# A wide convolution in an eight-sample audio network: three outputs from five products instead of two from four, with the side work of GpSimd and VectorE put in another order

## The reference, cut to what matters

```python
logits = conv1d_same(gelu(conv1d_same(xt, rc_w1, rc_b1)), rc_w2, rc_b2)    # the router
...
sh = conv1d_same(xt, sh_w1, sh_b1)        # 9 taps, 128 -> 512 channels
sh = jax.nn.silu(sh)
sh = conv1d_same(sh, sh_w2, sh_b2)        # 1 tap, 512 -> 128 channels
z = residual + y + sh.transpose(0, 2, 1)
return layer_norm(z) * ln_g + ln_b
```

## Time and profile before

| | us |
|---|---|
| median of 3 runs | 1534.27 |
| lowest, highest | 1530.68, 1536.31 |
| profiled execution, its own time | 1544.43 |
| its span in the trace | 1542.6 |
| TensorE busy (10360 records) | 1305.9, 85% of the span |
| VectorE busy | 1003.6, 65% |
| ScalarE busy | 644.9, 42% |
| GpSimd busy | 699.3, 45% |
| mean granted clock of TensorE | 0.92 |

### The profile page before, as it was taken

How to read it: one execution, slowest core, us unless ns; L and a number is a source line. 1 busy time by engine, 2 the same in 40 slices (tenths; PEclk the granted TensorE clock), 3 DMA queues, 4 the chain that set the end, 5 groups by cost and what they waited for, 6 DMA issues and landing times.

```text
span 1542.6 us, 33397 instructions
## 1 busy us (share of the span) xinstructions
PE 1305.9 (85%) x10360; PEld 1103.2 (72%) x10361; DVE 1003.6 (65%) x3235; ACT 644.9 (42%) x1610; POOL 699.3 (45%) x1055
## 2 busy tenths in 40 slices
PE   6696777787899937778899899988998989999974
PEld 3464646564899935556788778876887989999953
DVE  4467768665466656757863786467663628989946
ACT  1346272523122204335335453445334436666623
POOL 0112556444688853133531444242614526777732
PEclk9697989898999978989999899999998999999987
DMA  6000400003588840010010001000100237777725
GB/s 191 4 21 6 111 27 22 25 21 95 161 266 256 263 170 1 2 42 1 24 61 0 2 14 58 14 1 1 43 1 8 95 97 191 196 194 198 196 88 161
DMA packets 102202, 128.46 MB, mean 83 GB/s; under 512 B 21015, under 2 KB 61181, under 8 KB 101842
## 3 DMA queue, kind: packets, MB, share of 16 engines
q1 hardware_dynamic: 88786, 102.36, 23.1%
q0 software_dynamic: 13312, 24.74, 4.8%
HBM read 96.13 MB, written 34.94 MB: 85 GB/s over the span
## 4 chain that ended last, share of the span: by engine, by line
PE 60%; DVE 15%; issue 7%; DVEq 6%; POOL 5%; ACT 4%; DMA 2%; POOLq 0%; SPq 0%; ACTq 0%
PE psum L980 12%; PE psum L1133 11%; PE psum L989 9%; DVE work L1554 3%; PE psum L1142 3%; PE psum L1047 2%; POOL rows_in L2130 2%; PE psum L1094 2%; PE psum L1072 2%; PE psum L794 2%; PE psum L1191 2%; PE psum L969 2%; PE psum L1018 2%; DVE stats L1537 2%; PE psum L1067 1%
## 5 line engine op out<-in xcount | busy, mean ns | idle before, releaser
L1133 PE MATMUL psum<-NT,wreg 128*128 128x182 f32 (+1 forms) x1536 | 261.6, 326 | 10.2 <-ACT pack L1434 5.1
L1133 PEld LDWEIGHTS psum<-NT,wreg 128*128 128x128 f32 x1536 | 247.9, 192 | 18.9 <-ACT pack L1434 5.9
L2162 POOL DMA_INDIRECT rows_out<-work,expert_row_kept x208 | 206.2, 992 | 79.6 <-issue 41.1
L980 PE MATMUL psum<-work 128*128 128x128 f32 x1664 | 222.7, 277 | 0.9 <-ACT work L1336 0.9
L980 PEld LDWEIGHTS psum<-work 128*128 128x128 f32 x1664 | 203.9, 193 | 1.7 <-issue 0.9
L2111 POOL TENSOR_TENSOR rstd<-var_eps,pack 128x6 f32<-128x6 f32 x40 | 56.5, 1415 | 215.0 <-DVE var_eps L1544 214.9
L1329 ACT ACTIVATE work<-psum,work 128x128 f32<-128x128 f32 x416 | 118.6, 368 | 64.4 <-PE psum L980 64.3
L1876 DVE SCALAR_TENSOR_TENSOR work<-psum,work 128x128 f32<-128x128 f32 x416 | 117.1, 344 | 7.7
L794 PE MATMUL psum<-pack,work 128*128 128x128 f32 (+2 forms) x288 | 51.4, 336 | 82.0 <-DVE work L1554 75.5
L1885 DVE TENSOR_SCALAR work<-psum,expert_row_kept 128x128 f32<-128x128 f32 x208 | 72.8, 350 | 71.8 <-PE psum L969 36.6
L2130 POOL DMA_INDIRECT rows_in<-N,slot_now x96 | 100.5, 1046 | 28.6 <-issue 28.4
(11 more groups left out here) (364 smaller groups left out, 2894.3 us busy)
## 6 DMA issues: line engine op xcount, KB each, us to landing
work<-w_and_b SPq DMA_DIRECT2D x104, 258.0 KB
work<-in_ew SPq DMA_DIRECT2D x104, 256.0 KB
work<-rows_in SPq DMA_DIRECT2D x208, 65.0 KB
work<-rows_out SPq DMA_DIRECT2D x32, 384.0 KB, 4.2
rows_out<-work,expert_row_kept POOLq DMA_INDIRECT x208
work<-in_xT SPq DMA_DIRECT2D x8, 375.0 KB, 3.0
w_and_b<-in_ew SPq DMA_DIRECT2D x1, 2560.0 KB
out<-H SPq DMA_DIRECT2D x8, 320.0 KB
```

The costliest lines, as they stand in the source:

```text
L980: r_ = mm(v.ps1[:, c * P:(c + 1) * P], v.w1[:, c * P:(c + 1) * P], v.xT, start=True, stop=True)
L1133: r = mm(bank[:, half * HALF_PAIRS:half * HALF_PAIRS + p1 - p0], weights[:, m * P:(m + 1) * P], product_input(name, g, k, p0, p1), start=( ...
L2162: G.indirect_dma_start(rows_out[m], bass.IndirectOffsetOnAxis(ap=v.dest, axis=0), v.y, None, bounds_check=last, oob_is_err=False).then_inc ...
```

## The change

What it does, part by part:
- **Products.** For one group of three taps, three neighbouring outputs come from five products on a third of the columns. A unit is now one sample (748 outputs, 250 triples) and one block of hidden channels, thus 8 units. It is made of three fills: p12 (6 matmuls of 250 columns), p03 (6) and p4 (3). Fills take the two PSUM banks in turn.
- **Combination.** Seven operations of 250 columns on VectorE (four, a drain, three), where part p03 of the next unit stands. ACT copies 500, 500 and 250 columns, and silu works on 748 columns at once.
- **Rows.** Both halves of a sample are multiplied after its fourth block. Those of lane 1 stand at the end of an iteration.
- **Fills.** `FILL` changes at the end of the list, and parts are weighted by cost (6, 6, 3, and 4 for rows).
- **Input and weights on GpSimd.** `turn` becomes twelve operations, one of 504 and eleven of 252 columns, with three drains. `make_conv_weights` becomes eight operations of 1536 columns.
- **GpSimd's order.** The norm powers of norm5 come first in an iteration, and `turn` of lane 1 stands at the end of its own iteration. The norm powers of norm6 come ahead of rows 0 and 1. Rows 2 and 3 come last, after `add_b_sh2` of lane 0. The two scatters follow each other. `ln_b` is added in a step of its own.
- **Memory.** Half of the convolution's hidden rows now lie in `H`, where samples 0 and 1 stood. These are stored to DRAM once after iteration 0 and loaded back in the second experts' stage. The conv weights arrive in four DMAs instead of two.

```diff
-        UNIT = [(q, m) for q in range(UNITS) for m in range(4)]
+        UNIT = [(k, m) for k in range(LANES) for m in range(4)]
+        POINTS = {"p12": (1, 2), "p03": (0, 3), "p4": (4,)}
...
+        for k, m in UNIT:
+            PARTS.append(("p12", k, m))
+            if m == 1 and k > 0:
+                PARTS += [("rows", 2 * k - 2, 0), ("rows", 2 * k - 1, 0)]
+            PARTS += [("p03", k, m), ("p4", k, m)]
+        CONV_END = [("last", LANES - 1, 3), ("rows", UNITS - 2, 0), ("rows", UNITS - 1, 0)]
+        COST = {"p12": 6, "p03": 6, "p4": 3, "rows": 4}
...
-        FILL = [3, 1, 0, 0, 0, 0, 1, 0] + [0.5, 0.5] * TILES + [3.5, 2, 1.5, 1, 0.5]
+        FILL = [3, 1, 0, 0, 0, 0, 1, 0] + [0.5, 0.5] * TILES + [3.5, 2.5, 2, 1, 0]
...
+            sp.wait_ge(first_rows_final, 1)
+            sp.dma_start(first_rows_dram, first_rows).then_inc(first_rows_out, 16)
...
+                fill = f"{what}{m}_{k}"
+                bank = fill_bank(fill)
+                before, bi = fill_before(fill, i)
+                e.wait_ge(act_conv_done, act_conv.at("conv", before, 0, bi))
...
+                    for half, x in enumerate(POINTS[what]):
                         for g in range(3):
+                            r = mm(bank[:, half * TRIPLES:(half + 1) * TRIPLES], conv_w[:, x, g, k_cols(m)], turned(k)[:, x, g:g + TRIPLES],
+                                   start=(g == 0), stop=(g == 2))
...
+                V.scalar_tensor_tensor(conv_sum, p1, 3.0, p2, ALU.mult, ALU.add)
+                V.scalar_tensor_tensor(p2, p1, -3.0, p2, ALU.mult, ALU.add)
+                V.scalar_tensor_tensor(p0, p0, 3.0, p3, ALU.mult, ALU.add)
+                V.scalar_tensor_tensor(conv_p4, conv_p4, 1.5, p3, ALU.mult, ALU.add)
                 e.drain()
...
+                V.tensor_tensor(y[:, 0], p0, conv_sum, ALU.subtract)
+                V.scalar_tensor_tensor(y[:, 1], p3, 2.0, p2, ALU.mult, ALU.add)
+                V.scalar_tensor_tensor(y[:, 2], conv_p4, 4.0, conv_sum, ALU.mult, ALU.subtract
+                                       ).then_inc(dve_conv_done, dve_conv.step("conv", f"y{m}_{k}", 0))
...
+                if what == "p03" and 4 * k + m > 0:
+                    conv_combine(*UNIT[4 * k + m - 1], i)
...
+                G.tensor_tensor(s, w0, w4, ALU.add)
+                G.tensor_tensor(w3, w1, w1, ALU.add)
                 e.drain()
...
+                G.tensor_tensor(w2, s, w1, ALU.subtract)
+                G.tensor_tensor(w3, w3, w0, ALU.add)
                 e.drain()
...
+                G.tensor_tensor(w1, w1, s, ALU.add)
+                e.drain()
+                G.tensor_tensor(s, w4, w4, ALU.add)
+                e.drain()
+                G.tensor_tensor(s, s, s, ALU.add)
+                e.drain()
+                G.tensor_tensor(w3, w3, s, ALU.add)
                 e.drain().then_inc(conv_made, 1)
...
+                G.tensor_tensor(t[:, 3:5], x(3, 2), x(1, 2), ALU.subtract)
+                G.tensor_tensor(t[:, 0], x(0), x(2), ALU.subtract)
+                G.tensor_tensor(t[:, 1], x(1), x(2), ALU.add)
+                G.tensor_tensor(t[:, 2], x(1), x(2), ALU.subtract)
+                e.drain()
...
             def attention(i, first):
-                if not first:
-                    turn(1, i - 1)
                 for k in range(LANES):
                     rstd("attention", 5, k, i)
...
                     scatter(1, i - 1, [0])
-                    add_conv_rows(0, i - 1)
                     scatter(1, i - 1, [1])
-                    add_conv_rows(1, i - 1)
                 for k in range(LANES):
                     rstd("attention", 6, k, i)
                 if not first:
-                    add_conv_rows(2, i - 1)
+                    add_conv_rows(0, i - 1)
+                    add_conv_rows(1, i - 1)
                 turn(0, i)
+                for k in range(LANES):
+                    add_ln_b(k, i, first)
+                turn(1, i)
                 add_b_sh2(0, i)
                 if not first:
+                    add_conv_rows(2, i - 1)
                     add_conv_rows(3, i - 1)
```

More of the change, by code:

```diff
@@ L563, in audio_tower @@
[L563 removed]
+        for k, m in UNIT:
[5 more added lines that the diff above has]
+        COST = {"p12": 6, "p03": 6, "p4": 3, "rows": 4}
+        FILLS = [f"{x}{m}_{k}" for x, k, m in PARTS + CONV_END if x != "last"]
@@ L584, in interleaved @@
                 reached += FILL[x // LANES]
-                while conv and n * sum(FILL) * LANES < reached * len(PARTS) and n < len(PARTS):
+                while conv and n < len(PARTS) and sum(costs[:n]) * sum(FILL) * LANES < reached * sum(costs):
                     order.append(("conv", n, 0))
@@ L1145, in none @@
+                r.then_inc(pe_conv_done, pe_conv.step("conv", fill, 0))
             def none(k, i):
@@ new lines, in conv_silu @@
+            def conv_silu(k, m, i):
+                e.wait_ge(dve_conv_done, dve_conv.at("conv", f"y{m}_{k}", 0, i))
+                A(conv_h[m][:, 0:L], conv_h[m][:, 0:L], ACT.Silu, bias=w("b_sh1", (m, m + 1)), scale=1.0 / 6.0
+                  ).then_inc(act_conv_done, act_conv.step("conv", f"s{m}_{k}", 0))
+            def conv_part(n, i):
+                what, k, m = (PARTS + CONV_END)[n]
+                u = 4 * k + m
+                if what == "last":
+                    conv_silu(k, m, i)
+                    return
+                fill = f"{what}{m}_{k}"
+                bank = fill_bank(fill)
+                e.wait_ge(pe_conv_done, pe_conv.at("conv", fill, 0, i))
+                if what == "rows":
+                    q = k
@@ L1446, in conv_part @@
                     n_ = WIDTH[3 * (q % 2) + 2]
-                    nc.scalar.copy(conv_rows[q % 2][:, 0:2 * P], conv_bank[1][:, 0:2 * P])
-                    nc.scalar.copy(conv_rows[q % 2][0:n_, 2 * P:3 * P], conv_bank[1][0:n_, 2 * P:3 * P]
-                                   ).then_inc(act_conv_done, act_conv.step("conv", f"rows{q}", 0))
+                    nc.scalar.copy(conv_rows[q % 2][:, 0:2 * P], bank[:, 0:2 * P])
+                    nc.scalar.copy(conv_rows[q % 2][0:n_, 2 * P:3 * P], bank[0:n_, 2 * P:3 * P]
+                                   ).then_inc(act_conv_done, act_conv.step("conv", fill, 0))
+                    return
+                bk, bm, bi = unit_before(k, m, i, 2 if what == "p12" else 1)
+                e.wait_ge(dve_conv_done, dve_conv.at("conv", f"y{bm}_{bk}", 0, bi))
+                dst = {"p12": conv_p12[u % 2], "p03": conv_p03, "p4": conv_p4}[what]
+                nc.scalar.copy(dst, bank[:, 0:len(POINTS[what]) * TRIPLES]).then_inc(act_conv_done, act_conv.step("conv", fill, 0))
+                if what == "p4" and u > 0:
+                    conv_silu(*UNIT[u - 1], i)
             def attention(i, conv):
```

223 lines of the change are left out of this document (107 added, 116 removed).

## The result

The median of the changed kernel is 1560.0 us (4 runs, 1555.6 to 1565.3) against 1532.6 for the kernel before in the same job; the ratio is 1.0177, with a 95% interval of [1.0135, 1.0219]. The change is slower, clear of the noise. The forecast of 1524 had the wrong sign, and its range missed the result. The profiled execution took 1565.3 us with a span of 1563.2, 20.6 more than before. (The medians differ by 27.4: the profiled execution of the kernel before was some 12 us above its median, that of the changed kernel 5.

What follows compares the result with a forecast made beforehand. The prediction saw iterations and tail near TensorE's limit, with convolution filling waits for VectorE. Its terms, -3 - 9.3 + 1.6 - 5 + 8 - 3, gave -10.7 us from the profiled 1544.4, median 1534.3, so 1524 us, range 1496 to 1545.

Steps and rivals of the forecast that it cites:

- The sum: Whole kernel: -3 - 9.3 + 1.6 - 5 + 8 - 3 = -10.7 us, giving 1524 us.
- Products: Convolution on TensorE: 240 records per pair for 384, 10.2 us less each, 41 over four if nothing else ends later.
- my second rival: Filling only covers waits, so iterations and boundaries change by 0: 1534 us; chance 0.20.
- 46.6 us of which most is plain work: Output projection to the router's scores: the argument held against the claim that filling only covers waits.
- Chunks (-1 each): Lane 1's norm5T to output projection: -1 us per iteration up to the third chunk's cx, 0 behind it.
- Output projection to scores (-3.1 each): From output projection to the router's scores, with less filling: -3.1 us per iteration, -9.3 for three.
- End of the iteration (+0.8): Scores to lane 1's next norm5T: 32.5 us for 31.7, +0.8 twice, +1.6.
- First boundary (-5): Behind iteration 0: `turn` runs during TensorE's router work and no rows are added; -5 us, bounds -7 to 0.
- Weights (+8): Eight GpSimd weight operations instead of three, in iteration 0's unfilled chunks: +8 us, bounds +5 to +17.3.
- Tail (-3): Behind the last scores: 89.6 us for 92, counted as -3, bounds -12 to +4.
- a sign that it is wrong: Changed profile: iterations of 154 us, or none under 163, would disprove the forecast of about 160 us.
- The slow rival: GpSimd holds VectorE through weight operations (+17.3) and three iteration ends (+18), no first-boundary gain: 1554 us; chance 0.13.

Runs made afterwards that it cites:

- d4: Changed kernel with two of three products of each sum cut to 62 columns instead of 250: 1540.6 us, ratio 1.0031 to the kernel before.
- d1: Changed kernel with six of the combination's seven operations and one drain left out: 1522.7 us, ratio 0.9924 to the kernel before.
- r7: Changed kernel with norm6, norm powers, variances and norm5 early, and the first chunk's fill behind the second chunk's masks: 1638.3 us, ratio 0.9804 to the kernel before.
- r2: Changed kernel with both norm powers ahead of row blocks 2 and 3 and lane 1's variance early: 1639.7 us, ratio 0.9927 to the kernel before.
- d3: Changed kernel with five of the eight weight operations left out: 1556.3 us, ratio 1.0119 to the kernel before.
- d2: Changed kernel with ten of the turn's twelve GpSimd operations left out: 1551.9 us, ratio 1.0108 to the kernel before.
- the reordering: Changed kernel's operations reordered: norm6, norm powers, variances and norm5 early, first chunk's combination later; 1512.4 us, ratio 0.9850 to the kernel before.
- s1: Changed kernel with the combination's seven operations split over three places, two, two and three: 1666.8 us, ratio 1.0081 to the kernel before.
- c_after_again: Changed kernel once more, unchanged, on the third job's chip: 1671.7 us, ratio 1.0023 to the kernel before.
- b1: Kernel before with lane 1's turn and both norm powers ahead of row block 3 and lane 1's variance early: 1668.3 us, ratio 0.9992 to the kernel before.
- r1: Changed kernel with lane 0's norm6 right behind its variance, ahead of lane 1's output: 1638.8 us, ratio 0.9897 to the kernel before.

## Why the prediction was wrong

The sum took filling that leaves TensorE for time that leaves the iteration. It failed in three terms, each of them a wait of TensorE for VectorE that the sum let shrink or kept small.

**Products: the size right, the worth small.** 78 records in the tail took 16.61 us, 0.213 each for the 0.215 forecast. But d4 shows what columns are worth: with half of them gone an iteration gives back 7 to 9 of 26 us and is at 163.7, the number of before. Inside the iterations the filling mostly covers waits of the attention chain. That was my second rival, at 0.20; I held "46.6 us of which most is plain work" against it.

**Chunks (-1 each): +4.2 and +3.0** (in the last iteration +0.3). At the third chunk's cx, where the prediction cut, they are +3.8 and +2.6 in front of it and +0.4 behind it, where 0 was forecast. The failed step is "there the router's VectorE work orders it. But `ln_b`'s two additions leave the place in front of its combination: -1". I counted what left that place, not what grew there. The combination takes 2.7 us for 1.3, ahead of lane 1's context, and TensorE waits 1.84 us for that. Then VectorE makes the route's slots and the masks; before, a row product of 3.48 us stood on TensorE in that time (909.61), and now nothing does, so that TensorE waits 4.67 us, in d1 as well. Behind this wait the stretch to the third chunk takes 12.28 us at a mean clock of 0.87, for 10.74 at 1.00 before. r7 moved the fill and its combination and got 3 us back.

**Output projection to scores (-3.1 each): 0.** "Now out, statistics, one combination and norm6 bring it to 15.6" failed. That was counted from the projection's end; measured from there it is 17.1 (18.5 in the table, which counts from its start). The step leaves out what stands on VectorE ahead of lane 0's norm6 and sets its time: lane 1's output and variance, whose projection is 8 us later on TensorE. One combination in place of two saves nothing either, since it is as long as both were. With norm6 early it is 14.4 by the table. "Now 4 large and 3 small fills (14.3) stand beside these: 26.5" failed as well: 28.1, with 25.7 once the wait ahead of it is gone.

**End of the iteration (+0.8): +4.6 and +3.7.** The norm power came at 19.8 (forecast 21.5), the rows at 9.55 (9.6), and TensorE's wait in front of them is the 7 us foretold. What failed is "From there two combinations fewer stand ahead of norm5, a larger one follows": it stands ahead of lane 1's variance, waits there for its own copy, and the second power is 11.2 us behind the first. I had followed only the first power. r2 returns 3.7 us.

**First boundary (-5): -2.5.** `turn` was costed at 6.5 us; it takes 8.6 with VectorE idle (iteration 0) and 9.8 beside it. Its operations of 252 columns cost 0.60 to 0.79 us alone and up to 0.97 beside VectorE, not 0.5. **Weights (+8): +7.0**, right; d3 returns 6.8 of it. **Tail (-3): -3.2**, the size right. But products are not what it hangs on: with half of them gone the convolution ends only 3.3 us earlier and the experts' rows keep the tail at 89.9, while six operations of the combination fewer give 5.8.

**The sum.** The measured 20.6 us more and the forecast 10.7 us less lie 31 us apart. Iterations one and two are 12.8 and 10.1 us over the forecast, the last 4.6, start and end 3.5, the boundary and weights together 0.6. In the changed kernel no full iteration was under 163 us, which the prediction had named as a sign that it is wrong.

**The slow rival** said 1554 and was near the result, by luck: d2 and d3 do not bear out its cause. The turn is worth about 10 us and the weights 7 to 9, where it had 18 and 17.3. What the runs bear out is placement: the same cut of VectorE's work gives 39 us before the reordering and 12 after it, and the order alone is worth 50.

Beside `turn`, the combination's operations start 0.74 to 0.9 us apart, for 0.34 alone, and `turn`'s own take up to 0.97. The Trainium skill (SBUF — State Buffer, SBUF: two separate sides) gives the shared ports to one of the two for a whole instruction; the rows agree, and at the iteration's end the two alternate, at a cost to both. In s1 it is harder: one VectorE operation takes 3.38 us (1072.50) beside `turn`'s first four, which stand from 1072.85 to 1075.60 with no drain between them. Why it waits for all four there, no run shows. Where such meetings fall decides what they cost, but all of `turn` is worth less than the order is.

## What to carry to other kernels

Where one engine's work is filling between waits, most of what is saved on it comes back as waiting (here 17 to 19 of 26 us per iteration, by d4); test that by halving it before rewriting it. When small pieces of side work become a larger block, list for every place in the in-order program what stands right behind the block, for both lanes, and move the block behind it. An in-order program written for one balance has to be reordered for the next: the same operations in another order were worth 50 us, while the change that saved the columns had lost 27.

## What was not expected of the hardware

**Chips differ by 8%.** The kernel before took 1535, 1651, 1669 and 1534 us in the four jobs. What differs within the iterations is the first piece alone (85 against 111 us). On the slow chips TensorE has gaps there with no releaser in the profile, among the chunks' matmuls of 128x32; from c_after_again:

```profile
1001.78 0.44 PE L1101 MATMUL psum<-work 128*32 128x128 f32 x5 [0.97 <-issue]
1003.25 0.43 PE L1101 MATMUL psum<-work 128*32 128x128 f32 x4 [1.02 <-issue]
1004.71 0.28 PE L1101 MATMUL psum<-work 128*32 128x128 f32 x1 [1.03 <-issue]
```

In this iteration they stand between 1001.78 and 1029.56, and GpSimd issues its 24 scatters from 994.67 to 1027.4. In the whole first piece they sum to 13 us, and TensorE is busy for 10 us more, at a mean clock of 0.85 for 0.93. From 560 to 1330 us such waits sum to 38 us there (42 in b1) and to 2.5 on the first chip. The tail of the old products takes 113.4 us there (b1) and the changed one's 95.8, against 93.0 and 89.8: that is most of why the change is level there and 1.8% slower here. Why those chips do it is open.

**The clock.** From lane 0's norm6T to the scores TensorE is busy throughout in both orders and does the same work. But behind a wait of 3.94 us it takes 28.1 us at a mean clock of 0.91, a mix of the two levels 1.00 and 0.50, and with no wait in front it takes 25.7 us at 1.00 (after, and r1):

```profile
998.77:1026.85 28.08, 28.08 (x126) 21.16 (x127) 10.06 (x20) 13.99 (x23) 13.33 (x19) 0.91 0.00 1
```

```profile
1060.30:1086.00 25.70, 25.70 (x127) 19.09 (x126) 14.55 (x23) 14.21 (x24) 17.25 (x25) 1.00 0.00 1
```

Here a wait cost 2.4 us more than its length.

**A loop's turn.** VectorE starts an iteration 3.27 us behind its last combination of the one before (1038.67, no releaser). The same gap stands in the other kernels that were read there, the one before the change included, at 3.0 to 3.4 us. It is missing behind iteration 0, which stands outside the loop: there the first addition (695.44) follows at once.
